# Adding a block's two halves into one table, one behind the other, in the first mixture of experts

## The chip, the cores and the metric

The kernel runs on one core of a Trainium2 chip. The time is device microseconds of one execution of the whole program, median of several; lower is better. Engines are named TensorE (PE; its weight loads PEld), VectorE (DVE), ScalarE (ACT), GpSimd (POOL) and SyncE (SP). SyncE and GpSimd also issue the DMA transfers, each on a queue of its own; both queues are served by the same 16 DMA engines.

## The reference, cut to what matters

Four layers with residuals over 2048 tokens of width 512: graph attention, a mixture of experts, a graph product, a second mixture.

```python
x = x + gnn0(layernorm(x), adj, ...)
# first mixture: 8 experts, the best two of each token, weights normalised
cw = (one_hot(selected_experts, E) * routing_weights[..., None]).sum(axis=1)
a = silu(einsum('th,ehi->tei', x, w_gate)) * einsum('th,ehi->tei', x, w_up)
out = einsum('te,teh->th', cw, einsum('tei,eih->teh', a, w_down))
x = x + out
# graph product: adj @ (degree-normalised (adj + adj.T) / 2 + I) @ layernorm(x)
x = x + gnn1(layernorm(x), adj, adj)
x = x + ffn1(layernorm(x), ...)          # second mixture, with a capacity per expert
```

## The kernel before, in words

The program is a row of stages, each a block in which every engine has its own instruction stream, with a barrier at the end: attention, output projection, routing (`route`), the first mixture (`experts_gated`), the graph product in two stages (`symmetric_product`, then `product_route`), the second mixture (`experts_mlp`). The order on each engine is the order in which the code is written; nothing reorders it.

**First mixture.** Routing gives every (token, expert) pair a slot in the table `sent0`, grouped by expert and padded to 23 blocks (`NB0`) of 256 rows (`BR`). GpSimd first scatters the rows there (`dispatch_labelled`), each with its token number and weight as two further columns. Then 23 blocks run. For block p SyncE loads its 256 rows and its expert's three weight matrices (768 KB each) into one of two buffer sets; ScalarE and VectorE split each operand in a high and a low part; TensorE computes with three products for each pair (`three_pass`, L201 to L203) and then the down projection (L1357); VectorE scales the result by the token's weight into `y`, a buffer for two blocks of two halves (`SB` = 2) of 128 rows (L1450). Last, GpSimd adds each half to the token's rows in HBM by an indirect DMA with addition (L1322). The two halves go to two tables: half 0 to `total0`, which `route` has filled with x (its `spill`), half 1 to `extra0`, which was cleared during attention. A token can stand in both halves of a block, so the two tables let both additions be in flight at once; between blocks, GpSimd waits for both (`added[s]`, L1317 and L1318) and then raises `landed`.

`landed` holds back VectorE: in `take_labels` (L1420 to L1423) it may overwrite the token numbers of the buffer that block p + 1 uses only when the additions of block p - 1 have landed. This cast stands in VectorE's order behind the split of the rows (L1418) and ahead of the last weight split (`moe_wd_lo`, L1414) and of the scaling (L1450) that GpSimd's next addition waits for (`evac`). SyncE's loads of the block after next wait for the same cast (`told`) and for that weight split.

**Symmetric product.** For each of the 16 row tiles, SyncE loads the tile from `total0` (L1490) and from `extra0` (L1491, into a ring of 4 buffers), VectorE adds them (L1530, `joined`), takes mean and variance, normalises and splits in high and low part (L1533 to L1553). SyncE also loads two adjacency tiles for each step, GpSimd subtracts them (`sym_s`, L1511), and TensorE multiplies (L1585, L1586) in two halves of 16 steps: the first half follows the rows as they become ready, the second finds them all there.

**Clears.** During attention SyncE writes zeros to the tables of `tables` in `attention` (L654), a part with each head.

Of the kernel before, what the change touches and what calls it, by code (L numbers as in the profile page):

```python
# [11 lines left out]
ALU = mybir.AluOpType  # L12
# [59 lines left out]
def members(tiles):  # L72
    return range(tiles.start, tiles.stop)
# [1167 lines left out]

def experts_gated(nc, k, block_expert, wide, put_at, table, w_gate, w_up, w_down, totals, second):

# [5 lines left out]
    with ExitStack() as st:  # L1249
# [17 lines left out]
        told, landed, relabelled = (c.sem(n) for n in ("told", "landed", "relabelled"))  # L1267
        added = [c.sem(f"added{s}") for s in range(SB)]
        put = [[c.sem(f"put{q}_{g}") for g in range(4)] for q in range(TOPK)]
# [7 lines left out]
        with nc.Block() as block:  # L1277
# [34 lines left out]
            @block.gpsimd  # L1312
            def _(pool):
                dispatch_labelled(pool, wide, put_at, table, put, relabelled)
                for p in range(NB0):
                    if p:
                        for s in range(SB):  # L1317
                            pool.wait_ge(added[s], 16 * p)  # L1318
                        pool.sem_inc(landed, 1)
                    for s in range(SB):  # L1320
                        pool.wait_ge(evac, START + SB * p + s + 1)
                        pool.indirect_dma_start(out=totals[s], out_offset=bass.IndirectOffsetOnAxis(ap=token[:, p % 2, s:s + 1], axis=0),  # L1322
                                                in_=y[:, SB * (p % 2) + s, :], in_offset=None, compute_op=ALU.add).then_inc(added[s], 16)
                for s in range(SB):
                    pool.wait_ge(added[s], 16 * NB0)

# [133 lines left out]

def symmetric_product(nc, adjT_dram, adj, src, totals, rowsum, colsum, z_hi, z_lo, out):

# [3 lines left out]
    with ExitStack() as st:  # L1466
# [4 lines left out]
        z = c.sb("z", [P, R, D])  # L1471
        more = c.sb("more", [P, R, D])
        half_dinv, z_scale, mean, var, root, rstd, t, dinv, deg, some, deg_root = (
# [6 lines left out]
        made, high, low, kept = (c.sem(n) for n in ("made", "high", "low", "kept"))  # L1480
        joined = c.sem("joined")
        deg_ready, deg_rooted, dinv_ready, varied, rooted, ch_s = (
            c.sem(n) for n in ("deg_ready", "deg_rooted", "dinv_ready", "varied", "rooted", "chain"))
        with nc.Block() as block:
            @block.sync
            def _(sp):
                def row(j):
                    if j >= R:
                        sp.wait_ge(joined, j - R + 1)
                    sp.dma_start(src[:, j, :], totals[0][j * P:(j + 1) * P, :]).then_inc(row_in[j], 16)  # L1490
                    sp.dma_start(more[:, j % R, :], totals[1][j * P:(j + 1) * P, :]).then_inc(row_in[j], 16)  # L1491

# [21 lines left out]
            def _(dve):  # L1514
# [11 lines left out]
                for g, tiles in enumerate(JOINED):  # L1526
                    n = len(members(tiles))
                    for j in members(tiles):
                        dve.wait_ge(row_in[j], 32)
                        dve.tensor_tensor(src[:, j, :], src[:, j, :], more[:, j % R, :], ALU.add).then_inc(joined, 1)  # L1530
                    for j in members(tiles):
                        dve.wait_ge(joined, j + 1)
                        dve.bn_stats(bn[:, j, :], src[:, j, :]).then_inc(ch_s, 1)  # L1533
# [659 lines left out]
def graph_moe_kernel(nc, x, adj, W_seq, a1, a2, W_out, b_out, gate_w, w_gate, w_up, w_down, Wr, br, W1, b1, W2, b2, out):  # L2193
    rows0, rows1 = NB0 * BR, E * CAP

    def scratch(name, shape):
        return nc.dram_tensor(name, shape, F32, kind="Internal").ap()
    s1_rows = scratch("s1_rows", [H, N])
    sent0, total0, extra0 = scratch("sent0", [rows0, ROW]), scratch("total0", [N + P, D]), scratch("extra0", [N + P, D])
    sent1, tags1 = scratch("sent1", [rows1, D]), scratch("tags1", [rows1, 2])  # L2200
# [4 lines left out]
    with ExitStack() as st:  # L2205
# [9 lines left out]
        with ExitStack() as st1:  # L2215
# [5 lines left out]
            with ExitStack() as st2:  # L2221
# [7 lines left out]
                with ExitStack() as st3:  # L2229
# [6 lines left out]
                    with ExitStack() as st4:  # L2236
                        s1, s2 = (Ctx(nc, st4, "first").sb(n, [P, NT, H]) for n in ("s1", "s2"))
                        first = front(nc, k, adj, x, W_seq, a1, a2, seq, rowsum, isolated, mean, rstd, bn, adj8, mask, s1_row, vals,
                                      s1, s2, ea, eb, g, ns2, big_s2, s1_rows, adjT_dram, rows_in, spilled, done)
                    then = attention(nc, k, adj8, mask, s1_row, vals, seq, ea, eb, g, ns2, big_s2, s1_rows, [sent0, sent1, extra0], tags1,  # L2240
                                     [total0, total], rows_in, spilled, done, x, x_sb, x_in, W_out, w_out, w_in, colhalf)
# [3 lines left out]
            with ExitStack() as st2:  # L2245
                c2 = Ctx(nc, st2, "two")
                SPENT.extend((x_in, w_in))
                norm_stats(nc, "norm1", bn, mean, rstd)
                xn = rows
                route(nc, k, "route0", x_sb, mean, rstd, gate_w, xn, put_at, weight, block_expert, total0, wide[:, :, D:ROW])  # L2250
                experts_gated(nc, k, block_expert, wide, put_at, sent0, w_gate, w_up, w_down, [total0, extra0], weight[:, 1, :])
                recycle(nc)
                with ExitStack() as st3:
                    c3 = Ctx(nc, st3, "diffuse")
                    z_hi, z_lo = c3.sb("z_hi", [P, NT, D], F32R), c3.sb("z_lo", [P, NT, D], F32R)
                    symmetric_product(nc, adjT_dram, adj, x_sb, [total0, extra0], rowsum, colsum, z_hi, z_lo, rows)
                    product_route(nc, k, adjT_dram, rows, x_sb, z_hi, z_lo, Wr, br, xn, put_at, sent1, total, tag)
# [30 lines left out]
```

## Time and profile before

| | |
|---|---|
| median of 3 runs | 2196.76 us (2195.17 to 2202.2) |
| the profiled execution | 2201.98 us, its span 2200.2 us |
| busy in the span | TensorE 1950.8 us (89%), VectorE 1280.7 (58%), ScalarE 1101.2 (50%), GpSimd 468.4 (21%) |
| mean granted TensorE clock | 0.949 |
| first mixture's blocks | about 790 to 1113 us |
| symmetric product | 1120.7 to about 1275 us |

Busy time is a sum over stages with different limits, so a stage is read by itself: by what each engine does in it and by the wait that ends last. In the rows below, a time line reads: start (us from the span's start), duration, engine, source line, operation, output <- inputs, count, and in brackets how long the engine sat idle before it and who released it. "Landing" is the time from a DMA's issue until its completion is seen. In names, the buffer of `y` and of the rows is `one_seq`, x is `one_x`, `total0` and `total` are both `total`, `extra0` is `extra`. "POOLq" stands for GpSimd's queue of instructions, here for the raising of `landed`.

### The profile page before, as it was taken

The numbers are of one execution on the slowest core, as the hardware profiler recorded it, in microseconds if no ns is written. First come the engines' busy times: TensorE is split into PE (matmuls) and PEld (weight loads), VectorE is DVE, ScalarE is ACT, GpSimd is POOL, SyncE is SP. The second block draws the span as 40 slices with busy tenths as digits, with TensorE's granted clock in tenths as the row PEclk, the third lists the DMA queues.
The fourth block names the chain that finished last, engine by engine and source line by source line (L and its number), as shares of the span: only waits on it lengthen the run. The fifth ranks groups of instructions, "written<-read, shape, count | busy, mean of one in ns | idle before, by whom it ended". The sixth has DMA issues, their size and how long they took to land. (4 is left out here: it accounts for less than half of the span.)

```text
span 2200.2 us, 38541 instructions
## 1 busy us (share of the span) xinstructions
PE 1950.8 (89%) x15937; PEld 1714.8 (78%) x15941; DVE 1280.7 (58%) x1732; ACT 1101.2 (50%) x1182; POOL 468.4 (21%) x335
## 2 busy tenths in 40 slices
PE   4869999999987169999948979949999999999998
PEld 4859999999965069999936857638888888888886
DVE  7799988888656347777758033533434334344342
ACT  4699888886934135555412033224435344253441
POOL 2033222211120422222225401262101011011011
PEclk9979999999989679999979989969999999999999
DMA  6443333323202558888757322253334344353432
GB/s 249 155 164 122 117 108 122 117 83 31 98 6 77 196 183 252 250 250 250 186 168 257 122 77 77 75 150 121 103 119 133 98 134 128 106 138 93 125 104 109
DMA packets 154248, 300.01 MB, mean 136 GB/s; under 512 B 16091, under 2 KB 53083, under 8 KB 149968
## 3 DMA queue, kind: packets, MB, share of 16 engines
q1 hardware_dynamic: 135792, 262.30, 36.9%
q0 software_dynamic: 18336, 35.98, 7.7%
q8 instruction: 91, 1.49, 0.3%
q14 instruction: 29, 0.24, 0.0%
HBM read 227.23 MB, written 79.71 MB: 140 GB/s over the span
## 5 line engine op out<-in xcount | busy, mean ns | idle before, releaser
L823 PE MATMUL attn_acc<-heads_vals,gat_adj 128*128 128x99 bf16 x2048 | 284.6, 209 | 0.0
L2093 DVE TENSOR_TENSOR moe_w_lo<-moe_raw,moe_w_hi 128x2048 fp32r<-128x2048 f32 x64 | 146.8, 2293 | 234.6 <-ACT moe_w_hi L2050 234.6
L821 PE MATMUL attn_acc<-heads_vals,one_x 128*128 128x99 bf16 (+1 forms) x2048 | 240.9, 231 | 18.6 <-DVE one_x L735 13.2
L821 PE MATMUL attn_acc<-heads_vals,heads_mask 128*128 128x99 bf16 (+1 forms) x2048 | 238.5, 229 | 0.0
L2050 ACT CAST moe_w_hi<-moe_raw 128x2048 fp32r<-128x2048 f32 x64 | 122.2, 1909 | 207.8 <-PE moe_y_ps L2018 192.6
L688 ACT ACTIVATE heads_mask<-gat_s_row,heads_big_s 128x2048 fp8e4<-128x2048 f32 x104 | 197.8, 1989 | 35.3 <-PE attn_acc L823 35.3
L821 PEld LDWEIGHTS attn_acc<-heads_vals,one_x 128*128 128x128 fp8e4 x2048 | 197.9, 99 | 15.7 <-issue 15.3
L823 PE MATMUL attn_acc<-heads_vals,attn_below 128*128 128x99 bf16 x2048 | 204.9, 212 | 5.3 <-issue 5.3
L688 ACT ACTIVATE one_x<-gat_s_row,heads_big_s 128x2048 fp8e4<-128x2048 f32 x101 | 192.1, 1989 | 23.5 <-PE attn_acc L823 23.5
L821 PEld LDWEIGHTS attn_acc<-heads_vals,heads_mask 128*128 128x128 fp8e4 x2048 | 197.3, 98 | 5.5 <-issue 5.4
L201 PE MATMUL moe_h_ps<-moe_x_hi,moe_w_hi 128*128 128x512 f32 x512 | 200.1, 391 | 1.6 <-DVE moe_x_lo L2098 1.6
L203 PE MATMUL moe_h_ps<-moe_x_hi,moe_w_lo 128*128 128x512 f32 x512 | 199.9, 390 | 0.0
L202 PE MATMUL moe_h_ps<-moe_x_lo,moe_w_hi 128*128 128x512 f32 x512 | 199.9, 390 | 0.0
L823 PEld LDWEIGHTS attn_acc<-heads_vals,gat_adj 128*128 128x128 fp8e4 x2048 | 196.9, 96 | 0.0
L823 PEld LDWEIGHTS attn_acc<-heads_vals,attn_below 128*128 128x128 fp8e4 x2048 | 195.8, 97 | 0.0
L2018 PE MATMUL moe_y_ps<-moe_w_hi,moe_h_hi 128*128 128x512 f32 x496 | 193.7, 390 | 0.0
L2018 PE MATMUL moe_y_ps<-moe_w_hi,moe_h_lo 128*128 128x512 f32 x496 | 193.1, 389 | 0.0
L2018 PE MATMUL moe_y_ps<-moe_w_lo,moe_h_hi 128*128 128x512 f32 x496 | 192.9, 389 | 0.0
L2178 POOL DMA_INDIRECT total<-moe_y,moe_token x28 | 64.0, 2286 | 553.4 <-DVE moe_y L2117 452.9
L2103 DVE TENSOR_TENSOR moe_h_lo<-moe_hf,moe_h_hi 128x512 fp32r<-128x512 f32 x128 | 87.7, 689 | 138.6 <-ACT moe_h_hi L2065 138.6
L2062 ACT ACTIVATE moe_hf<-moe_h_ps,moe_b_col 128x512 f32<-128x512 f32 x128 | 88.0, 688 | 115.8 <-PE moe_h_ps L203 100.7
L1585 PE MATMUL sym_acc<-diffuse_z_hi,sym_s 128*128 128x512 f32 x256 | 104.4, 408 | 40.6 <-POOL sym_s L1511 26.7
(347 smaller groups left out, 4736.2 us busy)
## 6 DMA issues: line engine op xcount, KB each, us to landing
moe_raw<-in_L_ffn_W_dram SPq DMA_DIRECT2D x64, 1024.0 KB, 5.2
moe_wg<-in_L_ffn_w_gate_dram SPq DMA_DIRECT2D x23, 768.0 KB, 9.1
moe_wu<-in_L_ffn_w_up_dram SPq DMA_DIRECT2D x23, 768.0 KB, 10.7
moe_wd<-in_L_ffn_w_down_dram SPq DMA_DIRECT2D x23, 768.0 KB, 12.3
gat_s_row<-s_rows SPq DMA_DIRECT2D x16, 1024.0 KB, 6.4
sym_a<-in_adj_dram SPq DMA_DIRECT2D x32, 512.0 KB, 4.3
one_seq<-sent SPq DMA_DIRECT2D x23, 514.0 KB, 3.6
sent<-all_zeros SPq DMA_DIRECT2D x10, 1028.0 KB
```

What stands on the lines that cost most here:

```text
L201: pe.matmul(out, ah, bh, start=(j == 0), stop=False)
L202: pe.matmul(out, ah, bl, start=False, stop=False)
L203: mm = pe.matmul(out, al, bh, start=False, stop=(j == n - 1))
L688: act.activation(mask[u][:, j, :], s1_row[:, u, :], ACT.Sigmoid, bias=big_s2[:, j, h:h + 1], scale=BIG, saturate=False).then_inc(stepped, 1)
L821: mm = pe.matmul(o[:, 0:first], mask[u][:, j, cols], both[:, 0:first], start=(j == 0 and b % 2 == 0), stop=(j == NT - 1), skip_group_check ...
L823: mm = pe.matmul(o[:, 3 * C1:6 * C1], second, both[:, 3 * C1:6 * C1], start=False, stop=(j == NT - 1), skip_group_check=True)
L1585: pe.matmul(acc[b][:], lhs, z_hi[:, j, :], start=(j == 0), stop=False)
L2018: mm = pe.matmul(y_ps[s][:], a[n * MC + m][:, s * P:(s + 1) * P], b[(NC + n) % 2][:, m, :], start=(n == 0 and m == 0 and q == 0), stop=(n ...
L2050: act.copy(w_hi[n % 2][:], raw[:, n % R]).then_inc(w_high, 1)
L2062: act.activation(hf[:, m % 2, :], h_ps[m % 2][:], ACT.Gelu, bias=b1_col[:, bass.ds(e, 1), n * MC + m]).then_inc(act_done, 1)
L2093: dve.tensor_tensor(w_lo[n % 2][:], raw[:, n % R], w_hi[n % 2][:], ALU.subtract).then_inc(w_low, 1)
L2103: dve.tensor_tensor(h_lo[n * MC + m][:], hf[:, m % 2, :], h_hi[n * MC + m][:], ALU.subtract).then_inc(h_low, 1)
```

## The change

Half 1 of a block is added to `total0` too. Since both halves can hold the same token, GpSimd waits for the landing of half 0 before it issues half 1, and for the landing of half 1 before it raises `landed` and issues the next block's half 0; one semaphore counts all additions. `extra0` is gone, with its twelve clears during attention, its sixteen loads, the ring `more` and the sixteen additions on VectorE.

```diff
-        added = [c.sem(f"added{s}") for s in range(SB)]
+        added = c.sem("added")
...
                 for p in range(NB0):
-                    if p:
-                        for s in range(SB):
-                            pool.wait_ge(added[s], 16 * p)
-                        pool.sem_inc(landed, 1)
                     for s in range(SB):
+                        if SB * p + s:
+                            pool.wait_ge(added, 16 * (SB * p + s))
+                        if p and s == 0:
+                            pool.sem_inc(landed, 1)
                         pool.wait_ge(evac, START + SB * p + s + 1)
-                        pool.indirect_dma_start(out=totals[s], out_offset=bass.IndirectOffsetOnAxis(ap=token[:, p % 2, s:s + 1], axis=0),
-                                                in_=y[:, SB * (p % 2) + s, :], in_offset=None, compute_op=ALU.add).then_inc(added[s], 16)
-                for s in range(SB):
-                    pool.wait_ge(added[s], 16 * NB0)
+                        pool.indirect_dma_start(out=total, out_offset=bass.IndirectOffsetOnAxis(ap=token[:, p % 2, s:s + 1], axis=0),
+                                                in_=y[:, SB * (p % 2) + s, :], in_offset=None, compute_op=ALU.add).then_inc(added, 16)
+                pool.wait_ge(added, 16 * SB * NB0)
...
                 def row(j):
-                    if j >= R:
-                        sp.wait_ge(joined, j - R + 1)
-                    sp.dma_start(src[:, j, :], totals[0][j * P:(j + 1) * P, :]).then_inc(row_in[j], 16)
-                    sp.dma_start(more[:, j % R, :], totals[1][j * P:(j + 1) * P, :]).then_inc(row_in[j], 16)
+                    sp.dma_start(src[:, j, :], total[j * P:(j + 1) * P, :]).then_inc(row_in[j], 16)
...
                     for j in members(tiles):
-                        dve.wait_ge(row_in[j], 32)
-                        dve.tensor_tensor(src[:, j, :], src[:, j, :], more[:, j % R, :], ALU.add).then_inc(joined, 1)
-                    for j in members(tiles):
-                        dve.wait_ge(joined, j + 1)
+                        dve.wait_ge(row_in[j], 16)
                         dve.bn_stats(bn[:, j, :], src[:, j, :]).then_inc(ch_s, 1)
...
-                    then = attention(nc, k, adj8, mask, s1_row, vals, seq, ea, eb, g, ns2, big_s2, s1_rows, [sent0, sent1, extra0], tags1,
+                    then = attention(nc, k, adj8, mask, s1_row, vals, seq, ea, eb, g, ns2, big_s2, s1_rows, [sent0, sent1], tags1,
```

GpSimd's order in the first mixture, before, from the last dispatches on. The waits are named by the first function that had the semaphore: `front_pool_chain` and `front_weight_chain` are `added[0]` and `added[1]`, `moe0_evac` is `evac`.

```order
L1237 DMA sent<-one_seq,all_put_at 5888x514 [waits front_dve_chain]
L1237 DMA sent<-one_seq,all_put_at 5888x514 x3
L1322 DMA total<-one_seq,moe_token 2176x512 [waits moe0_evac]
L1322 DMA extra<-one_seq,moe_token 2176x512 [waits moe0_evac]
L1322 DMA total<-one_seq,moe_token 2176x512 [waits front_pool_chain,front_weight_chain,moe0_evac]
L1322 DMA extra<-one_seq,moe_token 2176x512 [waits moe0_evac]
```

The same place in the changed kernel, where `front_pool_chain` is `added`.

```order
L1237 DMA sent<-one_seq,all_put_at 5888x514 [waits front_dve_chain]
L1237 DMA sent<-one_seq,all_put_at 5888x514 x3
L1322 DMA total<-one_seq,moe_token 2176x512 [waits moe0_evac]
L1322 DMA total<-one_seq,moe_token 2176x512 [waits moe0_evac,front_pool_chain]
L1322 DMA total<-one_seq,moe_token 2176x512 [waits front_pool_chain,moe0_evac]
L1322 DMA total<-one_seq,moe_token 2176x512 [waits moe0_evac,front_pool_chain]
```

Before, only every second addition waits for a landing, and for that of both; now every addition but the first waits for the one ahead of it.

SyncE's order in the symmetric product, before, at the last of the four rows that are loaded ahead; `front_x_turned` is `joined`.

```order
L1490 DMA one_x<-total 128x512
L1491 DMA sym_more<-extra 128x512
L1500 DMA sym_at<-adjT_dram 128x1024
L1501 DMA sym_a<-in_adj_dram 128x1024
L1490 DMA one_x<-total 128x512 [waits front_x_turned]
L1491 DMA sym_more<-extra 128x512
```

The same place in the changed kernel, from the stage's start.

```order
L1482 UNCONDITIONAL_BRANCH [waits barrier_Pool_Activation_PE_DVE_SP_release]
L1485 DMA one_x<-total 128x512 x4
L1494 DMA sym_at<-adjT_dram 128x1024
L1495 DMA sym_a<-in_adj_dram 128x1024
L1485 DMA one_x<-total 128x512
```

The first adjacency tiles stand behind four row loads instead of eight, and the row loads wait for nothing any more.

## Rows read from the trace of the kernel before

**Rows 1.** Busy time by stretches: us, engines' busy us (instructions), granted clock, DMA share, GB/s
```profile
945.02:958.65 13.63, 13.63 (x100) 12.88 (x100) 10.14 (x15) 8.48 (x11) 3.11 (x2) 1.00 0.86 249
1132.80:1212.40 79.60, 66.38 (x256) 52.67 (x256) 67.90 (x113) 18.60 (x34) 40.40 (x19) 0.91 0.70 239
1212.40:1275.00 62.60, 58.32 (x256) 47.99 (x256) 8.08 (x15) 1.07 (x3) 26.39 (x15) 0.99 0.32 102
350.00:450.00 100.00, 100.00 (x1749) 100.00 (x1747) 90.93 (x51) 81.24 (x44) 20.26 (x14) 1.00 0.31 97
```

**Rows 2.** Waits, 1125 to 1213 us: who waited for whom, us, times, longest
```profile
PE sym_acc L1585 <- DVE diffuse_z_lo L1553: 13.0, 3, 4.6
```

**Rows 3.** Instructions in time, one block of first mixture: start, us; landing of 960.51's add
```profile
958.65 1.56 POOL L1322 DMA_INDIRECT total<-one_seq,moe_token  x1 [10.21 <-DVE one_seq L1450]
960.51 1.56 POOL L1322 DMA_INDIRECT extra<-one_seq,moe_token  x1 [0.30 <-issue]
DMA to landing us min/median/max: 9.2/9.2/9.2
969.75 0.17 DVE L1423 CAST moe_token<-one_seq 128x2 uint32<-128x2 f32 x1 [0.24 <-POOLq L1319]
969.85 1.76 DVE L1414 TENSOR_TENSOR moe_wd_lo<-moe_wd,moe_wd_hi 128x1536 fp32r<-128x1536 f32 x1
972.55 1.56 POOL L1322 DMA_INDIRECT total<-one_seq,moe_token  x1 [10.48 <-DVE one_seq L1450]
```

**Rows 4.** Waits, 800 to 1125 us: the token cast
```profile
DVE moe_token L1423 <- POOLq L1319: 1.6, 4, 0.6
```

**Rows 5.** Second mixture's adds in time, with landings of 1661.63's and 1678.4's
```profile
1661.63 3.16 POOL L2178 DMA_INDIRECT total<-moe_y,moe_token  x1 [64.94 <-DVE moe_y L2117]
DMA to landing us min/median/max: 6.5/6.5/6.5
1668.88 2.85 POOL L2178 DMA_INDIRECT total<-moe_y,moe_token  x1 [4.09 <-DMA total<-moe_y,moe_token]
L2178 POOL DMA_INDIRECT total<-moe_y,moe_token x1: 1547/1547/1547, 1678.4 to 1678.4; - x1
DMA to landing us min/median/max: 4.9/4.9/4.9
```

**Rows 6.** DMA issues and adds' landings, 800 to 1075 us: count, KB, us to landing
```profile
extra<-one_seq,moe_token POOLq DMA_INDIRECT x20, 8.4
L1322 POOL DMA_INDIRECT total<-one_seq,moe_token x20: 1555/1558/1599, 808.7 to 1067.7; - x20
DMA to landing us min/median/max: 7.4/7.9/9.4
```

**Rows 7.** The same, 1080 to 1115 us: software queue's share, first adds, second adds' landing
```profile
q0 software_dynamic: 864, 1.57, 35.1%
L1322 POOL DMA_INDIRECT total<-one_seq,moe_token x3: 1558/1558/1568, 1081.4 to 1106.5; - x3
DMA to landing us min/median/max: 4.5/4.7/4.9
DMA to landing us min/median/max: 4.9/5.1/5.6
```

**Rows 8.** Busy time by stretches, 12 us after 958.65's add
```profile
970.65:971.65 1.00, 1.00 (x11) 1.00 (x10) 1.00 (x2) 0.00 (x0) 0.00 (x0) 1.00 0.47 180
```

**Rows 9.** The joins: group; three in time; SyncE's issue of the first adjacency tile
```profile
L1530 DVE TENSOR_TENSOR one_x<-one_x,sym_more 128x512 f32<-128x512 f32 x16 | 17.4, 1136 | 0.3 <-DMA sym_more<-extra 0.3
1147.47 4.30 DVE L1530 TENSOR_TENSOR one_x<-one_x,sym_more 128x512 f32<-128x512 f32 x4
1164.08 6.13 DVE L1530 TENSOR_TENSOR one_x<-one_x,sym_more 128x512 f32<-128x512 f32 x4
1184.39 2.48 DVE L1530 TENSOR_TENSOR one_x<-one_x,sym_more 128x512 f32<-128x512 f32 x4
1124.90 0.43 SPq L1501 DMA_DIRECT2D sym_a<-in_adj_dram  x1
```

More of the change, by code:

```diff
@@ L1239, in dispatch_labelled, with experts_gated @@
                                     oob_is_err=False).then_inc(put[q][n // 4], 16)
-def experts_gated(nc, k, block_expert, wide, put_at, table, w_gate, w_up, w_down, totals, second):
+def experts_gated(nc, k, block_expert, wide, put_at, table, w_gate, w_up, w_down, total, second):
     SB = BR // P
@@ L1458, with symmetric_product @@
 JOINED = [slice(0, 1), slice(1, 2), slice(2, 4)] + FOURS[1:]
-def symmetric_product(nc, adjT_dram, adj, src, totals, rowsum, colsum, z_hi, z_lo, out):
+def symmetric_product(nc, adjT_dram, adj, src, total, rowsum, colsum, z_hi, z_lo, out):
     HB = NT // 2
@@ L1471, in symmetric_product @@
         z = c.sb("z", [P, R, D])
-        more = c.sb("more", [P, R, D])
         half_dinv, z_scale, mean, var, root, rstd, t, dinv, deg, some, deg_root = (
@@ L1480, in symmetric_product @@
         made, high, low, kept = (c.sem(n) for n in ("made", "high", "low", "kept"))
-        joined = c.sem("joined")
         deg_ready, deg_rooted, dinv_ready, varied, rooted, ch_s = (
@@ L2198, in graph_moe_kernel @@
     s1_rows = scratch("s1_rows", [H, N])
-    sent0, total0, extra0 = scratch("sent0", [rows0, ROW]), scratch("total0", [N + P, D]), scratch("extra0", [N + P, D])
+    sent0, total0 = scratch("sent0", [rows0, ROW]), scratch("total0", [N + P, D])
     sent1, tags1 = scratch("sent1", [rows1, D]), scratch("tags1", [rows1, 2])
@@ L2250, in graph_moe_kernel @@
                 route(nc, k, "route0", x_sb, mean, rstd, gate_w, xn, put_at, weight, block_expert, total0, wide[:, :, D:ROW])
-                experts_gated(nc, k, block_expert, wide, put_at, sent0, w_gate, w_up, w_down, [total0, extra0], weight[:, 1, :])
+                experts_gated(nc, k, block_expert, wide, put_at, sent0, w_gate, w_up, w_down, total0, weight[:, 1, :])
                 recycle(nc)
@@ L2255, in graph_moe_kernel @@
                     z_hi, z_lo = c3.sb("z_hi", [P, NT, D], F32R), c3.sb("z_lo", [P, NT, D], F32R)
-                    symmetric_product(nc, adjT_dram, adj, x_sb, [total0, extra0], rowsum, colsum, z_hi, z_lo, rows)
+                    symmetric_product(nc, adjT_dram, adj, x_sb, total0, rowsum, colsum, z_hi, z_lo, rows)
                     product_route(nc, k, adjT_dram, rows, x_sb, z_hi, z_lo, Wr, br, xn, put_at, sent1, total, tag)
```

## The prediction

> **What bounds the kernel now.** I read the page's busy times first; they only say that TensorE leads. Where it does, the busy time by stretches says [rows 1], and then I read the first mixture of experts (800 to 1115 us) instruction by instruction, since all waits that the change adds stand there. In the first mixture one block takes 13.63 us, and in such a stretch TensorE is busy all of it, at a granted clock of 1.00 (2.4 GHz), while VectorE has 10.1 us of work and the DMA engines are busy 0.86 of the time [rows 1]. So a block costs what TensorE costs, as long as nothing else takes longer than 13.63 us a block. In the first half of the symmetric product (1132.8 to 1212.4 us) it is another picture: TensorE 66.4 of 79.6 us, VectorE 67.9, clock 0.91, a mix of both levels [rows 1]; there the vector work on the rows is what TensorE waits for [rows 2].
>
> Behind TensorE, in the first mixture, stands a second ring of waits, and it is nearly as long. GpSimd issues the two scatter-adds of a block 1.86 us apart (958.65 and 960.51) [rows 3]; the second lands 9.2 us after its issue, at 969.71, and the token cast of VectorE (L1423), which must wait for both, runs at 969.75: the column in brackets says that it sat for the release of L1319 [rows 3]. From the cast the ring goes on: the last weight split (1.76 us), the scaling of the block's results, and at 972.55, 2.80 us after the cast, the next first scatter-add [rows 3]. In 4 of 22 blocks the cast waits at all, 1.6 us in total [rows 4]. So the ring is just hidden, with no slack to speak of. That is the fact on which the forecast rests.
>
> **Part 1, one table in the first mixture.** GpSimd now waits for the landing of the first half before it issues the second, and for the second before it raises `landed`. Behind that waiting instruction stand, on GpSimd, only the next scatter-adds; behind `landed` stands VectorE's token cast, behind that the weight split and the scaling of the block's results, behind these GpSimd's next scatter-add and SyncE's loads (they wait for `told`). It is a ring, so its length becomes the block's time once it is over 13.63 us. Its length: 2.80 us from cast to first issue, some 0.1 us from landing to cast (969.71 to 969.75) [rows 3], first landing, 0.75 us from a landing to the next issue that waited for it, second landing. The 0.75 is read in the second mixture, whose adds are already chained in this way: issue at 1661.63, landing 6.5 us later, next issue at 1668.88 [rows 5]. So ring = 3.65 + first landing + second landing, and the point from which it decides is a sum of landings of 9.98 us.
>
> The first landing is there to read: 7.9 us median, 7.4 to 9.4, over the 20 blocks whose weight loads run beside it [rows 6]. That it has the other add right behind it on the queue does not seem to be why it is long: in the three last blocks, where no weights are loaded, it takes 4.7 us with the other add behind it as ever [rows 7], and an add that is alone in the second mixture, at 1678.4, takes 4.9 us [rows 5]. What makes it long is then the block's 2.3 MB of weights, which SyncE issues in the same 2 us. I keep 7.9.
>
> The second landing, issued some 8.65 us after the first issue, is not in the trace. From above it is bounded by 8.4 us, the second add's median beside the weight loads [rows 6], from below by 4.7, the least median without them [rows 7]. Which is nearer? In the block shown, whose first add goes out at 958.65, the DMA engines' share falls to 0.47 in the stretch from 970.65 [rows 8], so they are through some 12.5 us after the first issue; by then they have done the block's loads and both adds. An add takes 2.0 us of all engines (without loads beside them six adds take 35.1% of 35 us) [rows 7]. With one add fewer in that time the engines are through with the loads some 2 us sooner, about 10.5 us after the first issue. The second add, issued at 8.65, has 1.56 us of GpSimd before it [rows 3], so it moves its data from 10.2 us on, when next to nothing is left beside it. So it is nearest to the unloaded rows: 5.1 us, the second add's median there [rows 7].
>
> The ring: 3.65 + 7.9 + 5.1 = 16.65 us. It shows on the blocks whose first add runs beside weight loads, 20 of them, from the first add at 808.7 to that of the twenty-first at 1081.4, 272.7 us before [rows 6, 7]. Now 20 x 16.65 = 333.0, and 1.5 more since the first block's add lands after 9.4: 334.5 us, that is **+61.8 us**. The last blocks have no loads beside them: 3.65 + 4.9 + 5.1 = 13.65, as long as TensorE's 13.63, so nothing there. At the end the two last adds land one after the other: 4.5 + 0.75 + 5.1 = 10.35 us after the last first issue, against 1.86 + 4.9 = 6.76 [rows 3, 7]: **+3.6 us**, bare, since the stage's closing barrier waits for it. TensorE and the others have time to spare in a ring of 16.65 us: if its pauses bring the granted clock down, as in the symmetric product's 0.91 [rows 1], that costs nothing before TensorE's 13.63 us have grown by 3.
>
> **Part 2, no second table in the symmetric product.** Sixteen additions go (17.4 us of VectorE, 1.1 us each) [rows 9], and sixteen loads of 256 KB, with SyncE's wait for a free buffer of the joined rows. TensorE waits for VectorE's rows 13.0 us in three waits [rows 2]. What is late next is TensorE itself: the second half's 16 tiles are 58.3 us of it [rows 1], so four take 14.6, and VectorE's rounds of four, 16.6 and 20.3 us from join to join (1147.47, 1164.08, 1184.39), become 12.3 and 14.2 without 4.30 and 6.13 us of joins [rows 9]. So all of the 13.0 goes. The start also moves: the first tile of the adjacency, which GpSimd and then TensorE wait for, is issued at 1124.90, behind eight row loads of the same length, 0.43 us and a little between them [rows 9]; with four it is issued some 1.9 us sooner. Sum **-15 us**, with bounds of 7 (half of it comes back as waits for the adjacency's tiles) and 20 (the joins' whole 17.4 and the start).
>
> **Part 3, the clears.** Twelve writes of zeros to the second table go from SyncE's queue during attention. TensorE is busy 100 of 100 us there [rows 1], so: nothing; at most a few tenths, either way.
>
> **Sum:** 61.8 + 3.6 - 15 = +50.4 us. The profiled execution took 2201.98 us (span 2200.2), 5.2 over the median of the runs, 2196.76; against that one 2252, against the median **2247 us**, which I give.
>
> Bounds of this case: first landing 7.4, second 4.7, gain 20: 20 x 15.75 + 1.5 - 272.7 + 3.6 - 20 = +27, 2224 us. Second landing half way to the loaded value (6.75), gain 7: 20 x 18.3 + 1.5 - 272.7 + 3.6 - 7 = +91, 2288 us.
>
> **The rivals.** *The ring stays hidden (faster).* If the first add lands late only because the second one shares its queue and its rows in memory, it would alone take what it takes unloaded, 4.7, and the ring 3.65 + 4.7 + 5.1 = 13.45 us, under TensorE's 13.63. Then only -15 + 3.6 = -11 us is left: 2185. It decides at 9.98 us for both landings. For it speaks that both adds do share the engines; against it that the first add, which is ahead on the queue, is as quick with the second behind it as alone when no weights are loaded [rows 5, 7]. The Trainium skill's page "DMA: Bandwidth & Descriptors", section "Anatomy of one DMA — SWDGE (gpsimd) path", would have this case: a transfer issued by GpSimd costs about 2.0 us plus its bytes at 436 GB/s, for 256 KB an estimated 2.6 us, two of them 5.2, well under 9.98. The trace disagrees: these adds take 4.5 us at the least [rows 7].
>
> *Partly relieved.* The first add lands after 6.5 us, the value in the second mixture at the start of a chain [rows 5], the second after 4.7: ring 14.85, 20 x 14.85 + 1.5 - 272.7 = +25.8, and +3.6 - 15 = +14: 2211 us.
>
> *Both adds loaded.* The loads, which now start later too, stretch beyond the second add's flight, and it takes 8.4: ring 19.95, +127.8 + 3.6 - 15 = +116: 2313 us. Against it: the loads' queue is fed at the same point of the ring as before, right ahead of the first add.
>
> **How the numbers follow.** The forecast 0.74, the hidden ring 0.08, partly relieved 0.10, both loaded 0.08. The range takes in the forecast's bounds and, to leave out less than 2 in 10, the partly relieved case: 2211 to 2288. A measurement of this kernel can tell about 0.3% (6.6 us) from no change. Faster by more than that: the hidden ring, less a little for a gain that shrinks: 0.07; within: the rest of it and the lower edge of the partly relieved case: 0.03; slower: 0.90.
>
> **What would show it.** In the trace after: the first adds of blocks 1 to 20 some 16.6 us apart instead of 13.63; the token cast waiting in every such block, about 5 us, for GpSimd's release line; first landings still near 8 us and second ones near 5; TensorE with idle time of about 3 us a block in 800 to 1150. In the symmetric product no join, no waits of TensorE for the low part of the rows, and its first half near 67 us instead of 79.6. I am wrong if the token cast waits no more than now, that is if the sum of both landings is under 10 us; the size is wrong if the second landing is near 8.

## The result, and the profile after

The changed kernel takes **2243.77 us** (median of 4 runs, 2241.27 to 2246.16), the kernel before 2195.97 beside it (2194.1 to 2202.2). The ratio is **1.0209**, with a 95% interval of 1.0194 to 1.0224: slower by 46 to 48 us (by the ratio, or by the two medians), where 50 were forecast (2247 us). The profiled execution of after took 2246.16 us, its span 2244.4, which is 44.2 us over that of before (2200.2). All times of after below are from this execution.

The ring of waits has become what bounds the first mixture. The busy time by stretches, for 15 of its blocks and then for the first half of the symmetric product, from TensorE's first instruction to the reading of its first results (columns as in [rows 1]):

```profile
839.80:1089.09 249.29, 219.33 (x1473) 197.66 (x1472) 148.47 (x211) 119.98 (x158) 46.66 (x31) 0.97 0.71 205
1188.24:1253.35 65.11, 60.26 (x244) 48.90 (x245) 49.52 (x94) 18.52 (x34) 37.29 (x18) 0.92 0.68 234
```

The second of these stretches in the trace of before:

```profile
1132.82:1209.18 76.36, 63.33 (x244) 50.47 (x245) 64.66 (x109) 18.60 (x34) 38.87 (x18) 0.90 0.70 241
```

In the first mixture TensorE used to be busy in all of a block, and the DMA engines for 0.86 of it [rows 1]. Now fifteen blocks take 249.29 us, 16.62 each, TensorE has 30 us of pauses in them, and the DMA share is 0.71. No engine is busy all the time: what sets the pace is a chain across engines, and a page of busy times does not show such a thing. The waits do (800 to 1180 us; who waited for whom, total us, times, longest):

```profile
POOL total L1322 <- DVE one_seq L1449: 170.2, 22, 27.3
POOL total L1322 <- DMA total<-one_seq,moe_token: 146.8, 24, 7.6
DVE moe_token L1422 <- POOLq L1320: 120.4, 21, 6.9
PE moe_y_ps L1356 <- DVE moe_h_lo L1430: 34.0, 31, 2.7
```

The third row answers to [rows 4]: the token cast waited 1.6 us in 4 blocks before, and waits 120.4 us in 21 blocks now, 5.7 each. The second is new. GpSimd waits in the ring for a landing (6.1 us each time) and for the scaling, by turns. TensorE's own wait is the fourth row, 34.0 us, one step behind the ring.

One turn of the ring in time, as in [rows 3] (start, us, engine, line, operation, idle before it and its releaser):

```profile
955.95 1.56 POOL L1322 DMA_INDIRECT total<-one_seq,moe_token  x1 [6.75 <-DVE one_seq L1449]
963.98 1.55 POOL L1322 DMA_INDIRECT total<-one_seq,moe_token  x1 [6.47 <-DMA total<-one_seq,moe_token]
969.85 0.17 DVE L1422 CAST moe_token<-one_seq 128x2 uint32<-128x2 f32 x1 [6.17 <-POOLq L1320]
969.94 1.76 DVE L1413 TENSOR_TENSOR moe_wd_lo<-moe_wd,moe_wd_hi 128x1536 fp32r<-128x1536 f32 x1
971.62 1.40 DVE L1449 TENSOR_SCALAR one_seq<-moe_y_ps,moe_weight 128x512 f32<-128x512 f32 x2
972.64 1.56 POOL L1322 DMA_INDIRECT total<-one_seq,moe_token  x1 [7.11 <-DVE one_seq L1449]
```

and the landings of its two adds, in the view of one line's instructions:

```profile
L1322 POOL DMA_INDIRECT total<-one_seq,moe_token x1: 1557/1557/1557, 955.9 to 955.9; - x1
DMA to landing us min/median/max: 7.8/7.8/7.8
...
L1322 POOL DMA_INDIRECT total<-one_seq,moe_token x1: 1553/1553/1553, 964.0 to 964.0; - x1
DMA to landing us min/median/max: 5.8/5.8/5.8
```

Read it as a sum: issue at 955.95, landing 7.8 us later at 963.75, second issue 0.23 behind it (0.27 by the trace's own times, since the view rounds a landing to 0.1 us), landing 5.8 us later at 969.78, cast at 969.85, the last weight split, the scaling, next issue at 972.64. That is 16.69 us, while TensorE's work of a block is 13.63 [rows 1].

Four points in time carry the whole difference:

```profile
806.12 1.60 POOL L1322 DMA_INDIRECT total<-one_seq,moe_token  x1 [27.27 <-DVE one_seq L1449]
...
1137.89 1.56 POOL L1322 DMA_INDIRECT total<-one_seq,moe_token  x1 [6.72 <-DVE one_seq L1449]
...
1178.19 0.17 DVE L1510 TENSOR_TENSOR sym_deg<-all_rowsum,all_colsum 128x16 f32<-128x16 f32 x1 [18.11 <-PEq L106]
...
1253.35 2.07 DVE L1548 SCALAR_TENSOR_TENSOR one_seq<-sym_acc,sym_half_dinv,one_seq 128x512 f32<-128x512 f32 x3 [11.53 <-PE sym_acc L1577]
```

The last two of them in the trace of before:

```profile
1120.77 0.17 DVE L1516 TENSOR_TENSOR sym_deg<-all_rowsum,all_colsum 128x16 f32<-128x16 f32 x1 [13.87 <-PEq L106]
...
1209.18 2.07 DVE L1557 SCALAR_TENSOR_TENSOR one_seq<-sym_acc,sym_half_dinv,one_seq 128x512 f32<-128x512 f32 x3 [8.21 <-PE sym_acc L1586]
```

From the first block's first add to that of the twenty-first: 331.8 us, 16.59 a block, against 272.7 before [rows 6, 7]: +59.1. The symmetric product's first instruction comes at 1178.19 instead of 1120.77: +57.4. From there to the reading of its first results: 75.2 us, against 88.4 before: -13.2. Together 57.4 - 13.2 = +44.2, the difference of the spans; the stages behind add nothing.

### The profile page after: what moved, and what is told of

Read it like the earlier page. It is cut to its first block and busy times, and to the rows that moved or that the text cites. A ratio compares the mean times of both kernels' runs of the same rounds, so it can differ in the third digit from the quotient of the medians.

```text
span 2244.4 us, 38519 instructions
## 1 busy us (share of the span) xinstructions
PE 1966.0 (88%) x15937; PEld 1718.2 (77%) x15941; DVE 1258.7 (56%) x1716; ACT 1103.0 (49%) x1182; POOL 464.9 (21%) x335
## 5 line engine op out<-in xcount | busy, mean ns | idle before, releaser
L821 PE MATMUL attn_acc<-heads_vals,one_x 128*128 128x99 bf16 (+1 forms) x2048 | 241.0, 231 | 18.5 <-DVE one_x L735 13.2
L1322 POOL DMA_INDIRECT total<-one_seq,moe_token x46 | 71.6, 1558 | 317.1 <-DVE one_seq L1449 170.2
## 6 DMA issues: line engine op xcount, KB each, us to landing
moe_wd<-in_L_ffn_w_down_dram SPq DMA_DIRECT2D x23, 768.0 KB, 10.9
```

The lines of the kernel that those rows point to most:

```text
L821: mm = pe.matmul(o[:, 0:first], mask[u][:, j, cols], both[:, 0:first], start=(j == 0 and b % 2 == 0), stop=(j == NT - 1), skip_group_check ...
L1322: pool.indirect_dma_start(out=total, out_offset=bass.IndirectOffsetOnAxis(ap=token[:, p % 2, s:s + 1], axis=0), in_=y[:, SB * (p % 2) + s, ...
```

## The experiments

All ratios are to the kernel before, run on the same chip beside each kernel.

**One part at a time: the chain alone.** The kernel before, with its two tables, joins and clears, and only the waits of the change: each half waits for the landing of the half ahead of it.

```diff
-                    if p:
-                        for s in range(SB):
-                            pool.wait_ge(added[s], 16 * p)
-                        pool.sem_inc(landed, 1)
                     for s in range(SB):
...
+                        if SB * p + s:
+                            pool.wait_ge(added[1 - s], 16 * (p + s))
+                        if p and s == 0:
+                            pool.sem_inc(landed, 1)
```

> The kernel before with the new waits alone: both tables, the joins and their loads stay, but each half's add waits for the landing of the half ahead of it. If the ring of two landings is the whole loss, the first adds of blocks 0 to 20 stand 16.6 us apart as in the changed kernel, the mixture is 59 to 62 us longer, and the time is about 2196 + 60 = 2256 us (ratio 1.027). If instead it matters that both halves go to the same table (the same rows of memory), the landings are shorter here and the time stays well under that, near 2196 in the extreme.

Measured: 2255.3 us, 1.027 (1.0253 to 1.0287), some 60 us slower. Its adds carry different names for the two tables, so the two landings can be read apart (DMA issues, 800 to 1138 us: count, median us to landing):

```profile
total<-one_seq,moe_token POOLq DMA_INDIRECT x20, 7.9
extra<-one_seq,moe_token POOLq DMA_INDIRECT x20, 5.7
```

Its waits from 800 to 1180 us:

```profile
POOL extra L1322 <- DMA total<-one_seq,moe_token: 140.2, 23, 7.1
DVE moe_token L1423 <- POOLq L1320: 119.5, 21, 6.9
```

The same waits as in after, with two tables. The first landing is 7.9 here too, though no other add is in flight beside it. So the price is that of the chain; that both halves go to the same table shows no part in it.

**The other part: no joins.** The kernel before, without the second table's loads and joins in the symmetric product (half 1's results are left out of the rows), the mixture untouched.

```diff
-                    if j >= R:
-                        sp.wait_ge(joined, j - R + 1)
                     sp.dma_start(src[:, j, :], totals[0][j * P:(j + 1) * P, :]).then_inc(row_in[j], 16)
-                    sp.dma_start(more[:, j % R, :], totals[1][j * P:(j + 1) * P, :]).then_inc(row_in[j], 16)
...
-                        dve.tensor_tensor(src[:, j, :], src[:, j, :], more[:, j % R, :], ALU.add).then_inc(joined, 1)
...
```

> The kernel before without the loads of the second table and the joining additions: the result leaves out every block's second half. If the symmetric product gains by itself, its first half becomes 13 us shorter and the time is 2183 us (ratio 0.994), with the first mixture as before. If that gain in the changed kernel came only because the stage started in another state (clock, queues), the time stays at 2196.

Measured: 2184.61 us, 0.9956 (0.994 to 0.9973). In its trace the stretch from the product's first instruction to the first results is this one (columns as above):

```profile
1116.71:1192.07 75.36, 60.51 (x244) 49.00 (x245) 57.15 (x124) 21.62 (x40) 40.08 (x19) 0.85 0.70 242
```

75.4 us against 88.4: the gain of 13 is there without the chain, as large as in after. The two parts add up: 1.027 and 0.9956 make +0.0226, the whole change +0.0209, inside the intervals. No run took out the clears, the third part, alone; what the two parts leave over, -0.0017 or some 4 us, is inside the intervals.

**What makes the first landing long.** After, with only a part of each weight matrix loaded from the third block on (0.64 MB a block instead of 2.3, the rest of the buffers stale).

```diff
-                def load_weights(p, r):
+                def load_weights(p, r, first=False):
...
+                        part = slice(None) if first else slice(0, 1)
+                        sp.dma_start(dst[:, part, :], src[bass.ds(ex, 1), :, :].rearrange("a (k q) i -> q (a k) i", q=P)[:, part, :]).then_inc(w_in[r], 16)
```

> The changed kernel, where from the third block on only the first quarter (for the down projection the first third) of each weight matrix is loaded, 0.64 MB a block instead of 2.3; the rest of the multiplications use old weights, so the result is another. If the first add lands late because of the weight loads beside it, it now lands after 5 to 5.5 us, the ring is 3.2 + 5.2 + 4.8 = 13.2 us, under TensorE's 13.63, the token cast hardly waits, and the time is about 2187 us (0.996). If its 7.9 us have another cause (the row loads, the place in VectorE's work), the blocks stay 16.6 us apart and the time stays at 2244 (1.021).

Measured: 2194.24 us (10 runs), 0.9993 (0.9983 to 1.0002). The loads that are left (DMA issues, 800 to 1085 us):

```profile
one_seq<-sent SPq DMA_DIRECT2D x20, 514.0 KB, 3.6
moe_wd<-in_L_ffn_w_down_dram SPq DMA_DIRECT2D x20, 256.0 KB, 5.4
moe_wg<-in_L_ffn_w_gate_dram SPq DMA_DIRECT2D x20, 192.0 KB, 4.7
moe_wu<-in_L_ffn_w_up_dram SPq DMA_DIRECT2D x20, 192.0 KB, 4.9
```

GpSimd's issues in time:

```profile
947.21 1.56 POOL L1323 DMA_INDIRECT total<-one_seq,moe_token  x1 [6.01 <-DVE one_seq L1450]
953.54 1.55 POOL L1323 DMA_INDIRECT total<-one_seq,moe_token  x1 [4.77 <-DMA total<-one_seq,moe_token]
961.23 1.56 POOL L1323 DMA_INDIRECT total<-one_seq,moe_token  x1 [6.14 <-DVE one_seq L1450]
```

The first landing falls to 6.1 us, the second to 4.7 (medians), the block to 14.0. The cause is right, its size was missed: I had set 5 to 5.5 for the first landing, which would have hidden the ring, and 514 KB of rows and 0.64 MB of weights still stretch it; 0.4 us a block over TensorE's 13.63 in 20 blocks makes the 7 us by which the time lies above the 2187 expected. So there are three doses: 4.7 us without loads [rows 7], 6.1 with 0.64 MB of weights, 7.9 with 2.3 MB. The ring's point of decision shows as well: landings of 6.1 + 4.7 = 10.8 us still cost 0.4 us a block. With the gap of 0.27 us that the next run deals with, the point lies at 10.5 and not at 9.98.

**The gap between a landing and the next issue.** In the mixture of after it is 0.27 us (0.26 to 0.27 in 20 blocks, by the trace's own times), where 0.75 was taken from the second mixture. There the instruction waits in another order. Here GpSimd waits first for the scaled half (`evac`), then for the landing:

```diff
-                        if SB * p + s:
-                            pool.wait_ge(added, 16 * (SB * p + s))
                         if p and s == 0:
+                            pool.wait_ge(added, 16 * SB * p)
                             pool.sem_inc(landed, 1)
                         pool.wait_ge(evac, START + SB * p + s + 1)
+                        if s:
+                            pool.wait_ge(added, 16 * (SB * p + s))
```

> The changed kernel with the two waits ahead of the second half's add in the other order: first for the scaled result, then for the landing, as the second mixture has them. There 0.75 us pass from a landing to the next issue, in the changed kernel's first mixture 0.23. If the order of the waits makes that difference, 0.5 us come back in each of 20 rings: 17.1 us a block and 2254 us (1.026). If the difference has another cause, the gap stays at 0.23 and the time at 2244 (1.021).

Measured: 2247.89 us, 1.0242 (1.0221 to 1.0262), where after has 1.0209 (1.0194 to 1.0224); the intervals touch. In time:

```profile
954.62 1.56 POOL L1323 DMA_INDIRECT total<-one_seq,moe_token  x1 [6.73 <-DVE one_seq L1450]
963.03 1.55 POOL L1323 DMA_INDIRECT total<-one_seq,moe_token  x1 [6.86 <-DMA total<-one_seq,moe_token]
971.08 1.56 POOL L1323 DMA_INDIRECT total<-one_seq,moe_token  x1 [6.49 <-DVE one_seq L1450]
```

The first of them lands after 7.7 us, at 962.30, and the second is issued 0.73 later (0.73 to 0.76 in 20 blocks): here the order of the waits alone reproduces the 0.75. But the second landing shrinks from 5.4 to 5.0 in the median, and the block takes 16.61 us, hardly more than after's 16.59; 17.1 was expected. So a delay there is for the most part given back. That an add which starts later has less of the weights' transfer left beside it would explain this; the run with the chain alone agrees, where the ten blocks with the longer first landings have second ones of 5.3 us in the mean, the other ten of 5.9.

**The ring taken out.** After, with four buffers of token numbers instead of two. The cast then waits for the landing of the block before last, and the ring spans two blocks.

```diff
-        weight, token = c.sb("weight", [P, 2, SB]), c.sb("token", [P, 2, SB], U32)
+        weight, token = c.sb("weight", [P, 2, SB]), c.sb("token", [P, 4, SB], U32)
...
-                    dve.wait_ge(landed, START + p - 1)
-                    dve.tensor_copy(token[:, r, :], x[:, SB * r:SB * r + SB, D]).then_inc(told, 1)
+                    dve.wait_ge(landed, START + p - 2)
+                    dve.tensor_copy(token[:, slot, :], x[:, SB * r:SB * r + SB, D]).then_inc(told, 1)
```

> The changed kernel with four buffers for the token numbers instead of two, so that the token cast of block p + 1 waits for the landings of block p - 2 instead of p - 1, and the scaling in the last block for those of the block two ahead; nothing else is changed, one table, chained adds. If the loss is the ring through the token cast, the ring has a whole block more of room, and what is left is GpSimd's own chain of 7.9 + 0.23 + 5.4 + 0.3 = 13.8 us, about TensorE's 13.63: the time is 2196 - 13 + 3 + 0 to 4, or 2186 to 2190 us (0.995 to 0.998). If the two landings in a row cost by themselves (the adds drift against the loads until both land after 8 us), GpSimd's chain is 16.5 us and more, and the time stays at 2244 or above.

Measured: 2190.16 us (12 runs, 2185.8 to 2215.62), 0.9977 (0.9949 to 1.0005). Fifteen blocks of its trace:

```profile
841.08:1045.26 204.18, 204.18 (x1470) 193.01 (x1469) 152.24 (x210) 117.71 (x158) 47.28 (x30) 1.00 0.85 250
```

GpSimd in the same stretch:

```profile
949.73 1.56 POOL L1322 DMA_INDIRECT total<-one_seq,moe_token  x1 [5.08 <-DMA total<-one_seq,moe_token]
956.63 1.58 POOL L1322 DMA_INDIRECT total<-one_seq,moe_token  x1 [5.34 <-DMA total<-one_seq,moe_token]
963.26 1.56 POOL L1322 DMA_INDIRECT total<-one_seq,moe_token  x1 [5.06 <-DMA total<-one_seq,moe_token]
```

TensorE is busy all the time at a granted clock of 1.00 (2.4 GHz), 13.61 us a block, as before, and no wait of the cast is left. So all that the change lost, it lost through this cast, though each of GpSimd's adds still waits for the one ahead. But GpSimd's chain is now as long as a block: from 949.73 to 963.26, two landings and two gaps, 13.5 us, and 13.8 in the next. It is as long as expected (13.8), but of other terms: its landings are 6.6 and 6.0 us in the median of 20 blocks, not 7.9 and 5.4, with the same 2.3 MB a block. In this run the last weight matrix is issued 3.7 us ahead of the block's first add, in after 1.8 us behind it (medians), so the add runs beside another part of the loads. That the sum came out was luck.

The same four buffers in the kernel before:

> The kernel before with four buffers for the token numbers. Its token cast waits 1.6 us in all, so at most that is to be had: 2194 to 2196 us (0.999 to 1.000), no difference. If the ring in the kernel before costs more than its visible waits, it is faster by more than 3 us.

Measured: 2197.1 us (12 runs; one of them took 4021.5 us, and nothing here shows why), 0.9992 (0.998 to 1.0004): no difference, as a ring that was hidden would have it [rows 4]. The four buffers are not worth anything by themselves.

The four buffers of after once more, to tell the gain from nothing:

> The same kernel as in the run with four token buffers, timed once more, since its interval there (0.9949 to 1.0005) just reaches no change. If one table with chained adds is worth the symmetric product's 13 us less some 3 at the mixture's end, the median is again 2186 to 2191 us and the interval ends below 1. If the gain was chance, it is at 1.000.

Measured: 2192.3 us (12 runs, 2185.97 to 2220.56), 0.999 (0.9963 to 1.0017). A gain over the kernel before is not shown. Of the 24 runs of this kernel, 19 lie between 2185 and 2196 us and 5 between 2213 and 2221; the two traces are of executions of 2188 us, so what those five lost is open. A chain with no time to spare, as read above, would do that, but no trace shows it.

**Both halves in flight, one table.** The section on the kernel before says that a token can stand in both halves of a block. For real rows that is too cautious: a block holds the rows of one expert, and a token goes to two different ones. Only padding rows (1792 of 5888) repeat, and they go to rows behind the N tokens. If the add skips those by a bound on its index, both halves may be in flight on one table, with the waits of the kernel before:

```diff
-        added = c.sem("added")
+        added = [c.sem(f"added{s}") for s in range(SB)]
...
+                    if p:
+                        for s in range(SB):
+                            pool.wait_ge(added[s], 16 * p)
+                        pool.sem_inc(landed, 1)
                     for s in range(SB):
-                        if SB * p + s:
-                            pool.wait_ge(added, 16 * (SB * p + s))
-                        if p and s == 0:
-                            pool.sem_inc(landed, 1)
...
+                                                in_=y[:, SB * (p % 2) + s, :], in_offset=None, bounds_check=N - 1,
+                                                oob_is_err=False, compute_op=ALU.add).then_inc(added[s], 16)
```

> One table as in the changed kernel, but both halves in flight at once as in the kernel before. A block holds the rows of one expert, and a token goes to two different experts, so a token never stands in both halves; only padding rows do, and these are skipped here by a bound on the row number (1792 of 5888 rows). If the chain is the whole loss and the joins the whole gain, the first mixture is as before (blocks 13.63 us apart, token cast waiting under 2 us) and the symmetric product 13 us shorter: 2183 us (0.994). If two adds into one table disturb each other in memory, landings grow beyond 8.4 us, the cast waits again and the time goes above 2196.

Measured: **2186.99 us, 0.9945 (0.9925 to 0.9966)**, 12 us quicker than the kernel before (2199.01 beside it): it beats both. GpSimd in time, with the token cast ahead of the last of its adds:

```profile
958.10 1.56 POOL L1322 DMA_INDIRECT total<-one_seq,moe_token  x1 [10.32 <-DVE one_seq L1451]
959.97 1.55 POOL L1322 DMA_INDIRECT total<-one_seq,moe_token  x1 [0.30 <-issue]
...
968.79 0.17 DVE L1424 CAST moe_token<-one_seq 128x2 uint32<-128x2 f32 x1 [0.41 <-POOLq L1319]
...
972.07 1.56 POOL L1322 DMA_INDIRECT total<-one_seq,moe_token  x1 [10.55 <-DVE one_seq L1451]
```

and the token cast's wait, 800 to 1130 us:

```profile
DVE moe_token L1424 <- POOLq L1319: 16.4, 10, 3.8
```

The issues are 1.87 us apart again, as in [rows 3]. But the cast waits 16.4 us where under 2 were expected: the ring comes up in ten blocks, and from 808.08 to 1085.05 a block takes 13.85 us instead of 13.63, 4 us in all. The rows above show what is longer: from cast to first add pass 3.28 us (968.79 to 972.07), where [rows 3] have 2.80. The bound is not free; with it an add goes out 0.5 us later, and that is enough to lift a ring with next to no slack over TensorE's 13.63. The landings have a part in it too: 8.3 and 8.5 us in the median, 7.9 and 8.4 before; whether the one table has to do with that is open. The symmetric product keeps its gain (74.7 us).

**The bound alone, with the chain of after:**

> The changed kernel, chain and all, with the same bound on the row number, so that padding rows are not added. If a landing's length is mostly waiting beside the weight loads and little its own rows, landings stay near 7.9 and 5.4 in full blocks and fall somewhat in padded ones: ring 15.5 to 16.6, time 2225 to 2244 us (1.013 to 1.021). If the bound alone explained the run with both halves in flight, this one would be near 2183 too.

Measured: 2246.57 us, 1.0222 (1.0203 to 1.0241), as slow as after and a little above the 2225 to 2244 expected. One line's instructions, 800 to 1140 us:

```profile
L1322 POOLq MOVE  x41: 29/29/29, 805.6 to 1137.2; - x41
L1322 POOL DMA_INDIRECT total<-one_seq,moe_token x41: 1553/1557/1598, 806.3 to 1138.0; - x41
...
DMA to landing us min/median/max: 2.7/5.0/9.2
```

Twenty blocks from 806.3 to 1138.0: 16.59 us each. That this is after's 16.59 again is luck: two things cancel. The bound puts a further instruction on GpSimd's queue ahead of each add (the MOVE above), and each add goes out 0.5 us later than in after: 0.75 us behind a landing instead of 0.27, 3.28 behind the cast instead of 2.79. So 15 of the 20 turns take 17.1 us in the mean, although in them the second landing falls to 4.8 in the median. The other five belong to the blocks whose second half is all padding: its landing falls to between 2.7 and 4.1, and their turns take 14.7 to 15.5. Why the bound costs the half microsecond was not tested. The bound alone brings nothing, so the gain of the version ahead comes from having no chain, not from writing less.

## Why the prediction was right, and where a term was off

**The bound of the kernel before: right.** The ring with no slack was the fact to find. The chain alone gives all of the loss, and with the cast's wait moved back by one block TensorE is busy all the time again.

**The ring's length: 16.65 forecast, 16.59 measured, with two terms off that cancel.** From cast to first issue 2.80 (2.79 in the turn shown): right. First landing 7.9: right (median 7.9, 7.3 to 8.9 in after's trace). The reason was right too: it is the weights beside it, not the second add behind it, since it stays 7.9 with no second add in flight, and falls with the weights. The gap from landing to issue, 0.75, was 0.5 too long: I took it from the second mixture's adds [rows 5], whose instruction waits in another order. The second landing, 5.1, was 0.3 to 0.4 too short: 5.4 in the median (5.0 to 6.3). It goes out earlier than I had it, by that same 0.5, and the last weight matrix lands 1.1 us sooner than before (10.9 us against 12.0, medians of 15), not the 2 us that I had for the engines being through with the loads; so the add still meets the end of the weights. The two errors hang together: swapping the waits brought both back near the forecast's values. So the sum came closer than its terms, and that is in part luck. The extra 1.5 us for a slow first landing did not come: that block took 16.67 us (806.12 to 822.79). Twenty blocks cost +59.1 instead of +61.8.

**The last blocks: "nothing there" was wrong by 2 us.** The adds at 1137.89, 1150.65 and 1160.99 are 23.1 us from first to last, the same blocks took 25.1 before [rows 7]. The ring had let TensorE run ahead of GpSimd: from 800 to 1180 us VectorE's scaling waits for TensorE only once, for 1.9 us, so the results lie there when the cast is through. With short landings the adds catch up, and the ring of 3.65 + 4.9 + 5.1, which I set equal to TensorE's block, takes 12.76 from 1137.89 to 1150.65. At the end the last two adds took 9.7 us instead of 10.35, +2.9 against [rows 3, 7]; +3.6 was forecast. The first add came 2.6 us earlier than in the trace of before; among the traces here it lies between 804.0 and 811.9 us, and I put no cause to it. All of it: -2.6 + 59.1 - 2.0 + 2.9 = +57.4.

**The granted clock: as said.** TensorE's pauses bring it down to a mean of 0.97, its work of a block goes from 13.63 to 14.6 us, and this is hidden behind 16.6. Its idle time is then 2.0 us a block, where about 3 were forecast.

**The symmetric product: -15 forecast, -13.2 measured; one step failed, and a gain that I did not have hides most of it.** The start moved by 2.0 us (10.05 us from the product's first instruction to TensorE's first, 12.05 before; 1.9 forecast). "All of the 13.0 goes" was 4.8 too much (waits from 1185 to 1257 us; compare [rows 2]):

```profile
PE sym_acc L1576 <- DVE diffuse_z_lo L1544: 4.8, 2, 4.6
```

The wait is TensorE's for the third row tile, whose low part is ready at 1202.3. I had looked at the rounds of four tiles, where VectorE is ahead once the joins are gone. The early rounds of one and two tiles have no such reserve, and there VectorE's instructions are sometimes stretched (time, VectorE):

```profile
1188.93 2.33 DVE L1540 TENSOR_SCALAR sym_z<-one_x,sym_mean,sym_z_scale 128x512 f32<-128x512 f32 x1
...
1196.25 1.46 DVE L163 TENSOR_TENSOR sym_t<-sym_rstd 128x2 f32<-128x2 f32 x1
...
1197.94 2.01 DVE L165 TENSOR_SCALAR sym_t<-sym_t 128x2 f32<-128x2 f32 x1
```

The same operations take 0.55, 0.16 and 0.17 us elsewhere in the traces. GpSimd's subtractions (L1505) run beside them: one from 1188.97 to 1190.99, one until 1197.69, one from 1197.93 to 1199.93, and the two last of VectorE's instructions end within 0.02 us of these, at 1197.71 and 1199.95. That the subtractions are the cause was not tested. The kernel without joins shows the same wait (5.2 us).

Waits and start then give 8.2 + 2.0 = 10.2 us. The other 3.1 are TensorE's own work, which no term of the forecast had: in the half it is busy 60.26 us instead of 63.33, at a granted clock of 0.92 instead of 0.90. Whether the clock is all of it is not shown.

**The clears: nothing that shows, as said.** The two parts measured leave a rest inside the intervals, and the first mixture's first add comes after 804.0 to 811.9 us in the four traces with the clears, after 804.9 to 808.1 in the seven without.

**The rivals.** The hidden ring fell: beside the weights the first add of a chain takes 7.9 us. With it fell the rule of the Trainium skill's page "DMA: Bandwidth & Descriptors", section "Anatomy of one DMA — SWDGE (gpsimd) path", that would have an add of 256 KB land after 2.6 us (an estimate from its figures): after has 4.5 at the least. "Partly relieved" fell too, since the landing at the start of a chain is 7.9 here; its second half, a short second landing, missed by 0.7. "Both loaded" fell at 5.4 against 8.4. Of the medians' difference, 47 to 48 us stand beside the forecast 50.4.

## What to carry to other kernels

Before a chain is lengthened, look for the instruction that waits for its end, and close the loop through the other engines: here a cast of 0.17 us of VectorE waited only 1.6 us in all, which meant a ring with no slack, and every further microsecond of it became time. A transfer's landing is read beside the loads that it will really have beside it, and a gap or a landing taken from another place is only worth what the waits there have in common with these. Where a serialising wait guards against two writers of the same row, look first whether the data can have two: that removed the table without the chain.

## What the runs showed of the hardware

- How long after a landing GpSimd's next DMA starts depends on what stands between: 0.27 us when the wait for the landing stands first and one already met behind it (after), 0.74 when the wait for the landing stands last (the run with swapped waits; the second mixture's 0.75 has that order too). The order is not all: with a bound on the row number it is 0.75 in after's order. Why was not tested.
- An accumulating scatter of 128 rows of 2 KB lands after 4.7 us alone. As the first add of a chain it took 6.1 beside 0.64 MB of weight loads, and 7.9 beside 2.3 MB; where these 2.3 MB were issued ahead of it (the run with four token buffers), 6.6.
- Little of that is the add's own rows. In the chain with the bound an add beside the 2.3 MB that moved 3 KB (1056.87) landed after 6.5 us, one of 40 KB (840.85) after 6.9, and those that moved all their 128 rows after 7.6 to 9.2. Without loads, one with nothing but padding lands after 2.7 us.
- The same loads land sooner when the two adds of a block are chained: the last weight matrix after 10.9 us in after, after 12.0 in the trace of before (medians of 15), after 10.7 in the run with the chain alone.
- In some blocks of after a pause of TensorE is followed by a stretch at the lower level of its clock. One such pause of 1.96 us ends at 959.14, and the granted clock goes as follows (after, columns as above):

```profile
958.00:960.00 2.00, 0.86 (x3) 0.73 (x4) 2.00 (x4) 1.09 (x3) 0.00 (x0) 0.86 0.71 221
960.00:962.00 2.00, 2.00 (x6) 1.46 (x5) 1.75 (x4) 0.98 (x2) 0.00 (x0) 0.50 1.05 261
962.00:964.00 2.00, 2.00 (x8) 1.60 (x7) 1.30 (x2) 1.72 (x2) 0.02 (x1) 0.78 1.07 327
964.00:966.00 2.00, 2.00 (x14) 1.81 (x14) 0.00 (x0) 0.00 (x0) 1.53 (x1) 1.00 1.07 403
```

At 0.50, that is 1.2 GHz, the matrix products of the down projection start 0.43 us apart, at 1.00 (2.4 GHz) 0.23. It was free here because TensorE's work of a block, 14.6 us with such stretches in it, stayed under the ring's 16.6.
